# A convolution of two layers computed as three short filters over even and odd blocks, in place of one filter of five slots

## The chip, the cores and the metric

The kernel runs on one core of one Trainium2 chip. The metric is the device time of one execution in microseconds; of three runs of the kernel before the median is 1592.81 us (1592.79 to 1595.31).

## The reference

```
for two layers (conditioned convolution, then a product over the feature dimension):
    out = x                                   # 64 batch entries, 64 channels, 1024 positions
    for typ in ('same', 'upsample', 'same', 'downsample'):
        s = style @ mw.T + mb                 # each batch entry has its own weights
        weight = SCALE * w * s ; weight = weight * rsqrt(sum(weight^2) + EPS)
        out = conv(out, weight) + b           # 3 taps; up by 2 then blur, blur then down by 2
    x = x + FFN(out)
layer 0: FFN(y) = y @ identity.T              # 1024 x 1024
layer 1: FFN(y) = y @ W_base.T + b_base + sum_e alpha_e * (y @ A_e.T @ B_e.T) * 2   # 4 experts, softmax gate
```

All is float32. Away from the ends of the 1024 positions, the four convolutions of one batch entry are together one linear filter, so they can be composed into one.

## The kernel before

The batch is worked in 32 pairs of entries (`j`), the two entries of a pair being halves `h` = 0 and 1. Two input rows, even and odd positions, lie over the 128 partitions (64 channels each): `xraw` holds x in partitions 0 to 63 and x moved by one position in 64 to 127, so every second column gives a pair of neighbouring positions. The output is laid out alike: a product of 128x128 with 512 columns gives all 1024 positions of a half.

Every float32 factor is split in a high part of the type float32r and the rest (`_h`, `_l`), and `three` (lines 1099 to 1101) issues three products: high by high, high by rest, rest by high.

For each pair TensorE composes the filter in stages, with ScalarE making the high parts and VectorE the low ones between them: `stage_v`, `stage_u`, `stage_t`. `stage_t` leaves five slots of 64 columns in PSUM for each half (`comp_ps[h]`). `t_high` (ScalarE, L509) and `t_low` (VectorE, L803, L976, L977) scale them by the style and place them in `tw[h]`: slot `u` is a matrix of 128x128 for shift `u`, whose second 64 columns are copies of the first, moved across the partitions. Then `stage_conv(j, h)` runs five slots, each `three` with 512 columns, over `x_h[h]`, `x_l[h]`. `x_h` is written by ScalarE (L488, `x_high`), `x_l` by GpSimd (L348, `split_low`). `conv_scaled` (ScalarE, L523) takes the result out of PSUM with scale and bias into `conv[h]`, GpSimd's `put_edge` (L355) writes the two positions at each end, which are computed apart in the prologue (`ends_0` to `ends_4`), and `stage_turn` (L1364) transposes it on TensorE for the FFN product.

What follows for each half:

```
for u in range(NSH):                                   # NSH = 5
    last = three(conv_ps[h][:, :], flat(tw[h][:, 0, u, :, :]), flat(tw[h][:, 1, u, :, :]),
                 x_h[h][:, u:u + HL], x_l[h][:, u:u + HL], u == 0, u == NSH - 1)
```

Each engine has its program written out by hand, and an engine works strictly in its own order, held by semaphores. TensorE's body for pair `j` puts the FFN products of pair `j-1` (`ffn_chunk`, 8 chunks x 2 column blocks in layer 0; `ffn_row`, 3 blocks in layer 1) between the composing stages of pair `j`, to give the other engines time: in layer 0 four times three products of 512 columns lie between `stage_t` and `stage_conv`, in layer 1 five times three of 354 or 352, and `stage_turn` is two times three (layer 0) behind the second half's convolution. VectorE's body is `compose_low` (`v_low`, `z_low`, `t_low`, `w2_low` for the next pair; in layer 1 also `gates`), then `turned_low`, `ffn_result` for pair `j-1`, `turned_low`.

In layer 0 the pairs 2 to 8 and the last carry one step each of layer 1's preparation: `prep(step)` on VectorE and ScalarE, `prep_between` and `prep_after` on TensorE. Before the loop of each layer stands a prologue, in which pair 0, the composing of pair 1, the ends and the transposed FFN weights (`turn_weights`, `fw_high`, `fw_low`) are interleaved.

SP issues all loads and stores of x: `load_x(j)` when `x_ready` says that pair `j-1` is split (xraw is a single buffer), then it waits for the FFN result of pair `j-2`, stores it and loads `xres` for `j-1`.

## Time and profile before

| | |
|---|---|
| profiled execution | 1594.2 us, its span 1592.3 us |
| median of the runs | 1592.81 us |
| TensorE busy | 1559.0 us, 98% |
| VectorE busy | 798.6 us, 50% |
| ScalarE busy | 577.3 us, 36% |
| GpSimd busy | 206.4 us, 13% |
| body of one pair | 22.47 us in layer 0, 23.50 us in layer 1 |

Busy time is time in which an engine has an instruction under way. Matmuls overlap in the records (a product starts before the one ahead of it has drained), so what a product costs in a run of them is the distance of their starts, not its length. A row of a timeline that stands for several instructions says xN; an idle time ahead of it is in brackets, with what ended it.

### The profile page before, as it was taken

How to read it: one execution, taken by the hardware profiler on the slowest of the kernel's cores; microseconds unless marked ns; L12 is line 12 of the kernel's file. 1: busy time of each engine (PE TensorE's matmuls, PEld its weight loads, DVE VectorE, ACT ScalarE, POOL GpSimd, SP SyncE). 2: the span in 40 equal slices, each digit the busy share in tenths (PEclk: the TensorE clock that was granted, in tenths of full speed). 3: DMA queues.
4: the chain of work that ended last, by engine and by line, in shares of the span. 5: the costliest groups of instructions: out<-in, count | busy, mean ns of one | idle time of the engine just before them, and what ended most of it. 6: DMA issues, size and time to landing. Idle time of an engine off the chain costs nothing.

```text
span 1592.3 us, 25445 instructions
## 1 busy us (share of the span) xinstructions
PE 1559.0 (98%) x8503; PEld 1376.3 (86%) x8503; DVE 798.6 (50%) x2061; ACT 577.3 (36%) x1291; POOL 206.4 (13%) x280
## 2 busy tenths in 40 slices
PE   5999999999999999999999999999999999999998
PEld 4688888888888888888868999999999999999998
DVE  7645655454444444454555554454555455445443
ACT  3323442334333333333333333333334333333332
POOL 1101010111011101111100110111111011011010
PEclk9999998999999999999999999999999999999999
DMA  4352332332333233333262333332332333333331
GB/s 103 99 117 82 106 80 64 95 101 83 102 83 105 81 104 79 105 92 92 66 185 67 79 96 88 79 105 79 83 101 79 99 85 89 96 79 99 86 79 66
DMA packets 54331, 145.66 MB, mean 91 GB/s; under 512 B 17233, under 2 KB 19345, under 8 KB 54306
## 3 DMA queue, kind: packets, MB, share of 16 engines
q1 hardware_dynamic: 53616, 144.96, 33.4%
q10 hardware_dynamic: 690, 0.37, 0.1%
q8 instruction: 15, 0.25, 0.1%
q14 instruction: 10, 0.08, 0.0%
HBM read 111.75 MB, written 33.55 MB: 91 GB/s over the span
## 4 chain that ended last, share of the span: by engine, by line
PE 93%; DVE 3%; issue 2%; DMA 1%; ACT 1%; POOL 0%; SPq 0%; DVEq 0%; POOLq 0%
PE bank L1099 29%; PE bank L1101 29%; PE bank L1100 28%; PE bank L1364 4%; PE bank L1246 1%; DMA xraw<-x_dram 1%; PE bank L1310 0%; PE bank L1281 0%; DVE fw_l L884 0%; DMA win<-in_L_cond_weights_dram 0%; PE bank L1176 0%; PE bank L1178 0%; PE bank L1300 0%; PE bank L1370 0%; DVE win L907 0%
## 5 line engine op out<-in xcount | busy, mean ns | idle before, releaser
L1099 PE MATMUL bank<-fw_h,ct_h 128*128 128x512 f32 (+2 forms) x1280 | 458.9, 358 | 0.6 <-DVE xout L856 0.5
L1100 PE MATMUL bank<-fw_l,ct_h 128*128 128x512 f32 (+2 forms) x1280 | 450.3, 352 | 0.0
L1101 PE MATMUL bank<-fw_h,ct_l 128*128 128x512 f32 (+2 forms) x1280 | 449.3, 351 | 0.0
L348 POOL TENSOR_TENSOR x_l<-xraw,x_h 128x512 fp32r<-128x512 f32 x128 | 165.8, 1317 | 1258.1 <-ACT x_h L488 1258.1
L992 DVE TENSOR_TENSOR ct_l<-bank,ct_h 128x384 fp32r<-128x384 f32 (+1 forms) x256 | 96.2, 417 | 390.3 <-ACT ct_h L536 389.8
L1101 PEld LDWEIGHTS bank<-fw_h,ct_l 128*128 128x128 f32 x1280 | 241.0, 188 | 22.7
L1099 PEld LDWEIGHTS bank<-fw_h,ct_h 128*128 128x128 f32 x1280 | 241.2, 188 | 20.8 <-issue 1.0
L1100 PEld LDWEIGHTS bank<-fw_l,ct_h 128*128 128x128 f32 x1280 | 241.6, 189 | 16.4
L1099 PE MATMUL bank<-x_h,tw 128*128 128x512 f32 x640 | 253.1, 395 | 0.5 <-DVE tw L977 0.5
L1101 PE MATMUL bank<-x_h,tw 128*128 128x512 f32 x640 | 252.8, 395 | 0.0
L1100 PE MATMUL bank<-x_l,tw 128*128 128x512 f32 x640 | 251.8, 394 | 0.0
L523 ACT ACTIVATE conv_buf<-bank,beta,lam 128x508 f32<-128x508 f32 x128 | 99.6, 778 | 400.1 <-PE bank L1101 400.1
L503 ACT ACTIVATE z_h<-bank,lam_pairs 64x256 fp32r<-64x256 f32 (+1 forms) x256 | 113.6, 444 | 214.1 <-PE bank L1101 194.9
L961 DVE TENSOR_SCALAR z_f<-bank,lam_pairs 64x256 f32<-64x256 f32 (+1 forms) x256 | 115.2, 450 | 146.4 <-PE bank L1101 138.7
L536 ACT CAST ct_h<-bank 128x384 fp32r<-128x384 f32 (+1 forms) x256 | 86.7, 375 | 174.4 <-PE bank L1246 61.6
L1101 PEld LDWEIGHTS bank<-x_h,tw 128*128 128x128 f32 x640 | 120.4, 188 | 27.9
L1099 PEld LDWEIGHTS bank<-x_h,tw 128*128 128x128 f32 x640 | 120.4, 188 | 27.9 <-DVE tw L977 0.9
L1100 PEld LDWEIGHTS bank<-x_l,tw 128*128 128x128 f32 x640 | 120.5, 188 | 27.4 <-issue 0.2
L803 DVE SCALAR_TENSOR_TENSOR tw<-bank,s_all,tw 128x320 fp32r<-128x320 f32 x128 | 70.5, 551 | 95.3 <-ACT tw L509 93.0
L856 DVE TENSOR_TENSOR xout<-bank,xres 128x352 f32<-128x352 f32 (+1 forms) x160 | 86.8, 576 | 40.9 <-PE bank L1246 40.9
L976 DVE CAST tw<-tw 64x640 fp32r<-64x640 f32 x128 | 88.8, 694 | 4.4
L488 ACT CAST x_h<-xraw 128x512 fp32r<-128x512 f32 x128 | 78.3, 660 | 4.8 <-DMA xraw<-x_dram 3.4
(203 smaller groups left out, 1783.1 us busy)
## 6 DMA issues: line engine op xcount, KB each, us to landing
xraw<-in_x_dram SPq DMA_DIRECT2D x32, 512.0 KB, 5.0
xres<-in_x_dram SPq DMA_DIRECT2D x32, 512.0 KB, 3.9
x_dram<-xout SPq DMA_DIRECT2D x32, 512.0 KB, 2.9
xraw<-x_dram SPq DMA_DIRECT2D x32, 512.0 KB, 5.0
xres<-x_dram SPq DMA_DIRECT2D x32, 512.0 KB, 3.9
out_dram<-xout SPq DMA_DIRECT2D x32, 512.0 KB, 2.9
xraw<-in_x_dram SPq DMA_DIRECT2D x32, 511.5 KB, 6.5
xraw<-x_dram SPq DMA_DIRECT2D x32, 511.5 KB, 6.5
```

The source lines that it names most:

```text
L348: nc.gpsimd.tensor_tensor(x_l[h][:, PAD:PAD + HL], src, x_h[h][:, PAD:PAD + HL].bitcast(F32), ALU.subtract).then_inc(s["x_ready"], 1)
L488: nc.scalar.copy(x_h[h][:, PAD:PAD + HL], xraw[:, h, :].rearrange("p (m q) -> p m q", q=2)[:, :, 0]).then_inc(s["x_hi"], 1)
L503: nc.scalar.activation(z_h[half(i), h, 0:4 - i, :], u_ps[half(h), i::2, :], ACT.Copy, scale=lam1_pairs[half(h), bass.ds(j, 1)]).then_inc(s ...
L523: nc.scalar.activation(conv[h][:, 2:HL - 2], conv_ps[h][:, 2:HL - 2], ACT.Identity, scale=lam4[:, bass.ds(2 * j + h, 1)], bias=beta[:, bas ...
L536: nc.scalar.copy(ct_h[:, ks, h, :], conv_ps[h][:, :].rearrange("p (k o) -> p k o", o=C)[:, ks, :]).then_inc(s["ct_hi"], 1)
L856: v.tensor_tensor(xout[:, lo:hi], ffn_ps[e][:, skip:skip + hi - lo], xres[:, lo:hi], ALU.add).then_inc(s["ffn_out"], 1)
L961: v.tensor_scalar(z_f[half(i), h, 0:4 - i, :], u_ps[half(h), i::2, :], lam1_pairs[half(h), bass.ds(j, 1)], None, ALU.mult).then_inc(s["z_o ...
L976: v.tensor_copy(tw[h][half(1), :, :, 1, :], tw[h][half(0), :, :, 0, :].bitcast(F32))
L992: v.tensor_tensor(ct_l[:, ks, h, :], conv_ps[h][:, :].rearrange("p (k o) -> p k o", o=C)[:, ks, :], ct_h[:, ks, h, :].bitcast(F32), ALU.su ...
L1099: mm(out, wh, xh, start=start, stop=False, skip_group_check=True)
L1100: mm(out, wh, xl, start=False, stop=False, skip_group_check=True)
L1101: return mm(out, wl, xh, start=False, stop=stop, skip_group_check=True)
```

## The change

The filter of five slots on 512 columns is computed in the way of a fast two-part filter. The 512 columns are taken as even and odd ones (256 each). Three short filters are run, each over 256 columns:

- P: the sum filter, slots `G0`, `G1` (sums of neighbouring slots) and 4, over the odd columns `o` (nine products into `comp_ps[h]`, the bank which held the composed slots).
- over the difference `d[:, 0]` of neighbouring columns, slots 0, 2, 4 (nine products into the first half of `conv_ps[h]`).
- over `d[:, 1]`, slots 1 and 3 (six products into the second half).

The even output columns are P plus the second result, the odd ones P minus the third. So:

- `tw` has 8 slots for 5; three of them are sums of neighbouring slots. VectorE now makes the scaled slots in float32 (`t_f`, which lies in the buffer `conv[h]`), adds, subtracts ScalarE's high part, and makes all copies between the partition halves. It does the first two steps for both halves before the others.
- GpSimd makes the differences (`neighbours`) ahead of ScalarE's high part, and the low parts of both `d` and `o`. It does this for pair `j+1` once the filters of pair `j` are ready; the edges of pair `j` go first.
- ScalarE makes the high parts of `x` for pair `j+1` in two pieces, around `sum_scaled`, which takes P out of PSUM with scale and bias into every second column of `conv[h]`. VectorE's new `conv_out` adds the other two results.
- In VectorE's body `conv_out(j, 0)` stands ahead of `w2_low` and `prep(step)`, `conv_out(j, 1)` behind them; in layer 1 `gates` stands ahead of both.
- TensorE waits for P scaled ahead of `stage_v(1)` and `stage_u(1)` in the prologue. Semaphores of the ends are merged.

```diff
 # VectorE
                 def t_low(j):
                     for h in range(2):
+                        full = t_f[h]
+                        dve.wait_ge(s["t_acc"], 2 * j + h + 1)
+                        v.tensor_scalar(full[:, 0:NSH, :], comp_ps[h][:, 0:NSH * C].rearrange("p (u c) -> p u c", c=C),
+                                        s_all[:, 0, bass.ds(2 * j + h, 1)], None, ALU.mult).then_inc(s["g_made"], 1)
+                        dve.wait_ge(s["g_made"], 4 * j + 2 * h + 1)
+                        v.tensor_tensor(full[:, G0:SLOTS, :], full[:, 0:3, :], full[:, 1:4, :], ALU.add).then_inc(s["g_made"], 1)
+                    for h in range(2):
                         dve.wait_ge(s["t_hi"], 2 * j + h + 1)
-                        low(tw[h][:, 1, :, 0, :], comp_ps[h][:, 0:NSH * C].rearrange("p (u c) -> p u c", c=C),
-                            s_all[:, 0, bass.ds(2 * j + h, 1)], tw[h][:, 0, :, 0, :]).then_inc(s["t_lo"], 1)
+                        v.tensor_tensor(tw[h][:, 1, :, 0, :], t_f[h][:, :, :], tw[h][:, 0, :, 0, :].bitcast(F32),
+                                        ALU.subtract).then_inc(s["t_lo"], 1)
                         dve.wait_ge(s["t_lo"], 2 * j + h + 1)
                         v.tensor_copy(tw[h][half(1), :, :, 1, :], tw[h][half(0), :, :, 0, :].bitcast(F32))
-                        v.tensor_copy(tw[h][half(0), :, 1:NSH, 1, :], tw[h][half(1), :, 0:NSH - 1, 0, :].bitcast(F32)
-                                      ).then_inc(s["t_ready"], 1)
+                        v.tensor_copy(tw[h][half(0), :, 1:NSH, 1, :], tw[h][half(1), :, 0:NSH - 1, 0, :].bitcast(F32))
+                        v.tensor_copy(tw[h][half(0), :, G0:SLOTS:G1 - G0, 1, :],
+                                      tw[h][half(1), :, 0:GM + 1:GM, 0, :].bitcast(F32)).then_inc(s["t_ready"], 1)
+                def conv_out(j, h):
+                    dve.wait_ge(s["p_scaled"], 2 * j + h + 1)
+                    dve.wait_ge(s["conv_acc"], 2 * j + h + 1)
+                    even = conv[h][:, 2:HL - 2:2]
+                    stt(out=conv[h][:, 3:HL - 1:2], in0=conv_ps[h][:, QL + 1:2 * QL - 1], scalar=neg4[...],
+                        in1=even, op0=ALU.mult, op1=ALU.add)
+                    stt(out=even, in0=conv_ps[h][:, 1:QL - 1], scalar=lam4[...],
+                        in1=even, op0=ALU.mult, op1=ALU.add).then_inc(s["c_mid"], 1)
...
                 def body(j, step=None, composed=False):
                     if not composed:
-                        compose_low(j, ly["lora"])
-                    elif ly["lora"]:
+                        compose_low(j)
+                    if ly["lora"]:
                         gates(j - 1)
+                    conv_out(j, 0)
+                    if not composed:
+                        w2_low(ly, j + 1)
                     if step is not None:
                         prep(step)
+                    conv_out(j, 1)
                     turned_low(j, 0)
 # GpSimd
+                def neighbours(j):
+                    pool.wait_ge(s["x_load"], 32 * j + 32)
+                    for h in range(2):
+                        m0, m1 = (xraw[:, h, at:at + L].rearrange("p (n e q) -> p e n q", e=2, q=2)[:, :, :, 0] for at in (0, 2))
+                        nc.gpsimd.tensor_tensor(d_f[h][:, :, :], m0, m1, ALU.subtract).then_inc(s["d_made"], 1)
+                def split_low(j):
+                    for h in range(2):
+                        pool.wait_ge(s["x_hi"], 2 * j + h + 1)
+                        nc.gpsimd.tensor_tensor(d_l[h][:, :, 1:QL + 1], d_f[h][:, :, :], d_h[h][:, :, 1:QL + 1].bitcast(F32),
+                                                ALU.subtract)
+                        nc.gpsimd.tensor_tensor(o_l[h][:, 1:QL + 1], xraw[:, h, 2:L:4], o_h[h][:, 1:QL + 1].bitcast(F32),
+                                                ALU.subtract).then_inc(s["x_ready"], 1)
+                def body(j, last=False):
+                    pool.wait_ge(s["t_ready"], 2 * j + 2)
+                    edges(j)
+                    if not last:
+                        x_next(j)          # waits t_ready again, then neighbours(j + 1), split_low(j + 1)
 # ScalarE
+                def x_high(j, h, first=False):
+                    if not first:
+                        act.wait_ge(s["conv_acc"], 2 * j + h - 1)
+                    act.wait_ge(s["d_made"], 2 * j + h + 1)
+                    nc.scalar.copy(o_h[h][:, 1:QL + 1], xraw[:, h, 2:L:4])
+                    nc.scalar.copy(d_h[h][:, :, 1:QL + 1], d_f[h][:, :, :]).then_inc(s["x_hi"], 1)
+                def sum_scaled(j, h):
+                    act.wait_ge(s["p_acc"], 2 * j + h + 1)
+                    nc.scalar.activation(conv[h][:, 2:HL - 2:2], comp_ps[h][:, 1:QL - 1], ACT.Identity, ...
 # body of ScalarE: v_high, z_high, t_high, (gate_exp), sum_scaled(j,0), w2_high, x_high(j+1,0), prep, sum_scaled(j,1), x_high(j+1,1), ...
 # TensorE
+                    for i, slot in enumerate((G0, G1, 4)):
+                        last = conv_tap(h, comp_ps[h][:, 0:QL], slot, o_h[h][:, i:i + QL], o_l[h][:, i:i + QL], i == 0, i == 2)
+                    last.then_inc(s["p_acc"], 1)
                     if not first:
                         pe.wait_ge(s["ct_ready"], 4 * j)
-                    for u in range(NSH):
-                        last = three(conv_ps[h][:, :], flat(tw[h][:, 0, u, :, :]), flat(tw[h][:, 1, u, :, :]),
-                                     x_h[h][:, u:u + HL], x_l[h][:, u:u + HL], u == 0, u == NSH - 1)
+                    for i, slot in enumerate((0, 2, 4)):
+                        conv_tap(h, conv_ps[h][:, 0:QL], slot, d_h[h][:, 0, i:i + QL], d_l[h][:, 0, i:i + QL], i == 0, i == 2)
+                    for i, slot in enumerate((1, 3)):
+                        last = conv_tap(h, conv_ps[h][:, QL:2 * QL], slot, d_h[h][:, 1, i:i + QL], d_l[h][:, 1, i:i + QL], False, i == 1)
```

## Rows read from the trace of the kernel before

**Rows 1.** The page: busy time and share by engine; the chain that ended last.
```profile
PE 1559.0 (98%) x8503; PEld 1376.3 (86%) x8503; DVE 798.6 (50%) x2061; ACT 577.3 (36%) x1291; POOL 206.4 (13%) x280
...
PE bank L1099 29%; PE bank L1101 29%; PE bank L1100 28%; PE bank L1364 4%; PE bank L1246 1%; DMA xraw<-x_dram 1%; PE bank L1310 0%; PE bank L1281 0%; DVE fw_l L884 0%; DMA win<-in_L_cond_weights_dram 0%; PE bank L1176 0%; PE bank L1178 0%; PE bank L1300 0%; PE bank L1370 0%; DVE win L907 0%
```

**Rows 2.** View by stretches: length, busy us (instructions) per engine, clock, DMA share, GB/s.
```profile
500.86:523.33 22.47, 22.47 (x116) 18.79 (x115) 10.14 (x24) 8.28 (x18) 3.12 (x4) 1.00 0.34 93
1196.49:1219.99 23.50, 23.50 (x143) 22.11 (x142) 11.78 (x33) 8.64 (x21) 3.11 (x4) 1.00 0.33 89
```

**Rows 3.** Timeline of TensorE, both layers: start, length, engine, line, tile.
```profile
507.70 0.28 PE L1100 MATMUL bank<-z_l,w_h 128*128 128x256 f32 x1
...
508.88 0.28 PE L1101 MATMUL bank<-z_h,w_l 128*128 128x256 f32 x1
...
511.55 0.19 PEld L1099 LDWEIGHTS bank<-x_h,tw 128*128 128x128 f32 x1
...
511.78 0.39 PE L1099 MATMUL bank<-x_h,tw 128*128 128x512 f32 x1
...
518.49 0.39 PE L1101 MATMUL bank<-x_h,tw 128*128 128x512 f32 x1
...
520.11 1.04 PE L1364 MATMUL bank<-ident,conv_buf 128*128 128x128 f32 x8
...
1210.32 0.39 PE L1099 MATMUL bank<-x_h,tw 128*128 128x512 f32 x1
```

**Rows 4.** Timeline of VectorE, then ScalarE, in the same bodies.
```profile
509.81 0.92 DVE L976 CAST tw<-tw 64x640 fp32r<-64x640 f32 x1
510.74 0.44 DVE L977 CAST tw<-tw 64x512 fp32r<-64x512 f32 x1
...
511.79 0.49 DVE L976 CAST tw<-tw 64x640 fp32r<-64x640 f32 x1
512.29 0.42 DVE L977 CAST tw<-tw 64x512 fp32r<-64x512 f32 x1
...
521.26 1.02 DVE L992 TENSOR_TENSOR ct_l<-bank,ct_h 128x384 fp32r<-128x384 f32 x2 [7.90 <-ACT ct_h L536]
...
507.04 1.22 ACT L488 CAST x_h<-xraw 128x512 fp32r<-128x512 f32 x2
508.57 0.53 ACT L509 ACTIVATE tw<-bank,s_all 128x320 fp32r<-128x320 f32 x1 [0.30 <-PE bank L1101]
...
1207.47 0.53 ACT L509 ACTIVATE tw<-bank,s_all 128x320 fp32r<-128x320 f32 x1 [0.33 <-PE bank L1101]
```

**Rows 5.** Groups by line and shape: count | busy, mean ns | idle before, releaser.
```profile
L348 POOL TENSOR_TENSOR x_l<-xraw,x_h 128x512 fp32r<-128x512 f32 x128 | 165.8, 1317 | 1258.1 <-ACT x_h L488 1258.1
...
L803 DVE SCALAR_TENSOR_TENSOR tw<-bank,s_all,tw 128x320 fp32r<-128x320 f32 x128 | 70.5, 551 | 95.3 <-ACT tw L509 93.0
...
L961 DVE TENSOR_SCALAR z_f<-bank,lam_pairs 64x256 f32<-64x256 f32 x128 | 61.8, 483 | 142.3 <-PE bank L1101 138.7
...
L966 DVE TENSOR_TENSOR z_l<-z_f,z_h 128x256 fp32r<-128x256 f32 x128 | 48.7, 422 | 2.2
```

**Rows 6.** Stretches of VectorE's `prep` steps 0, 2, 3, 6; last, one at start.
```profile
111.69:115.49 3.80, 3.77 (x11) 1.00 0.96 194
161.27:170.22 8.95, 5.37 (x17) 1.00 0.37 76
183.93:190.17 6.24, 5.82 (x18) 1.00 0.57 115
263.96:274.18 10.22, 7.37 (x14) 1.00 0.37 75
76.00:80.00 4.00, 2.90 (x6) 0.57 0.70 202
```

**Rows 7.** Timelines in the two prologues: VectorE, ScalarE.
```profile
48.69 0.22 DVE L746 TENSOR_TENSOR beta<-blur_n,bias 128x64 f32<-128x64 f32 x1
...
803.81 1.21 ACT L488 CAST x_h<-xraw 128x512 fp32r<-128x512 f32 x2 [3.39 <-DMA xraw<-x_dram]
```

More of the change, by code:

```diff
@@ L215, in build @@
         names = ("w_load mw_load params f_load0 f_load1 f_load2 f_load3 modt_acc modt s_acc s_ready w2_acc w2_ready d_acc dvar_ready dsqrt "
[L216 to L219 removed]
+                 "wt_acc wt_ready ends_in ends_acc "
+                 "edge_ready bias_acc bias_ready fw_acc fw_hi fw_ready chain "
+                 "x_load res_load d_made x_hi x_ready w2_hi w2_low v_acc v_hi v_ready u_acc z_hi z_own z_ready t_acc g_made t_hi "
+                 "t_ready blur_ready base_ready w1_placed mst_ready split_hi split_ready t_lo p_acc p_scaled conv_acc c_mid c_edge ct_acc ct_hi ct_ready ffn_acc ffn_out stored").split()
         for n, ly in enumerate(layers):
@@ L374, in _ @@
                                             ALU.subtract).then_inc(s["split_ready"], 1)
-                body(0, True)
-                with pool.Fori(1, NPAIR) as j:
+                neighbours(0)
+                split_low(0)
+                x_next(0)
+                pool.wait_ge(s["edge_ready"], 1)
+                if ly is not layers[0]:
+                    pool.wait_ge(layers[0]["s"]["ct_acc"], 2 * NPAIR)
+                edges(0)
+                with pool.Fori(1, NPAIR - 1) as j:
                     body(j)
+                body(NPAIR - 1, True)
         @block.scalar
@@ L480, in fw_high @@
                         nc.scalar.copy(dst, bank[6 + g % 2][:, :].rearrange("p (k e) -> p k e", k=4)).then_inc(s["fw_hi"], 1)
-                def x_high(j, first=False):
-                    act.wait_ge(s["x_load"], 32 * j + 32)
+                def x_high(j, h, first=False):
                     if not first:
-                        act.wait_ge(s["conv_acc"], 2 * j)
-                    for h in range(2):
-                        nc.scalar.copy(x_h[h][:, PAD:PAD + HL],
-                                       xraw[:, h, :].rearrange("p (m q) -> p m q", q=2)[:, :, 0]).then_inc(s["x_hi"], 1)
+                        act.wait_ge(s["conv_acc"], 2 * j + h - 1)
+                    act.wait_ge(s["d_made"], 2 * j + h + 1)
+                    nc.scalar.copy(o_h[h][:, 1:QL + 1], xraw[:, h, 2:L:4])
+                    nc.scalar.copy(d_h[h][:, :, 1:QL + 1], d_f[h][:, :, :]).then_inc(s["x_hi"], 1)
                 def v_high(j):
@@ L580, in _, with body @@
                 t_high(1)
-                def body(j, step=None, composed=False):
+                def body(j, step=None, composed=False, last=False):
                     if not composed:
-                        compose_high(j, ly["lora"])
-                    elif ly["lora"]:
+                        compose_high(j)
+                    if ly["lora"]:
                         gate_exp(j - 1)
-                    conv_scaled(j, 0)
+                    sum_scaled(j, 0)
+                    if not composed:
+                        w2_high(ly, j + 1)
+                    if not last:
+                        x_high(j + 1, 0)
                     if step is not None:
                         prep(step)
-                    conv_scaled(j, 1)
+                    sum_scaled(j, 1)
+                    if not last:
+                        x_high(j + 1, 1)
                     if ly["lora"]:
@@ L1035, in _ @@
                     prep_bias(ly, link, 2)
+                    conv_out(0, 0)
                     g = 6
@@ L1044, in _ @@
                     ends_0()
+                    conv_out(0, 0)
                     fw_low(0, 2)
@@ L1051, in _ @@
                 fw_low(g, g + 2 + 2 * n)
+                conv_out(0, 1)
                 g += 2 + 2 * n
@@ L1347, in stage_t, with conv_tap @@
                         last.then_inc(s["t_acc"], 1)
+                def conv_tap(h, out, slot, xh, xl, start, stop):
+                    return three(out, flat(tw[h][:, 0, slot, :, :]), flat(tw[h][:, 1, slot, :, :]), xh, xl, start, stop)
                 def stage_conv(j, h, first=False):
```

140 lines of the change are left out of this document (67 added, 73 removed).

## The prediction

> **What bounds the kernel now.** I read four views. The page's first part has TensorE busy 98% of the span, VectorE 50%; its chain of waits runs 93% through TensorE, 86% on the lines of `three` [rows 1]. The view by stretches says the same of one pair of batch entries: TensorE is busy for all of a 22.47 us body of layer 0 and a 23.50 us body of layer 1, VectorE for 10.14 and 11.78 us [rows 2]. So TensorE work taken out is time won, unless something late leaves a gap. The timelines show how late things are. In layer 0 ScalarE takes up the first composed filter (`t_high`) at 508.57; call that T. TensorE loads the first filter slot for the convolution at 511.55 (T+2.98) and multiplies at 511.78 (T+3.21), without a gap [rows 3]. VectorE finished this filter's last copy, `tw` L977, at 510.74+0.44 = 511.18, T+2.6 [rows 4]. The filter chain is thus early by under 0.4 us. In layer 1 T is 1207.47 and the first multiply is at 1210.32, T+2.85 [rows 3, 4].
>
> **TensorE: what goes.** The thirty 512-column products of a pair start from 511.78 to 518.49, 29 steps: 0.2313 us each. In a run of 256-column products, 507.70 to 508.88, ten steps take 1.18 us: 0.118 each [rows 3]. Before, a half costs 15 x 0.2313 = 3.47 us; after, eight slots of three products, 24 x 0.118 = 2.83. Saved: 0.638 x 128 halves = **-81.6 us**. Weight loads (0.19 us in the records) start every 0.118 us in that same stage and hold nothing up, so their number, 24 for 15, is free here; if forty-eight in a row did not keep that pace, at 3.47/24 = 0.145 us each the whole gain would be gone. I take 0.118: it is the same shape. The low end of the saving is therefore zero, the high end this.
>
> **VectorE: the filter chain (`t_low`).** It now does, in this order: scale slots of half 0 out of PSUM (128x320), add three slots (128x192), the same for half 1, and only then for half 0 subtract (128x512), copy 64x1024, 64x512, 64x256. Prices [rows 5]: ops with a pointer scalar out of PSUM are 0.483 at 256 columns and 0.551 at 320, so 0.55, and the slope is 1.06 ns a column; the two-tensor op is 0.422 at 256 columns, with that slope 0.35 for 192 and 0.69 for 512. Casts undisturbed are 0.42 for 512 and 0.49 for 640 [rows 4], slope 0.55 ns, so 0.70 for 1024 and 0.28 for 256. The Trainium skill (VectorE: DVE Perf Modes, the TRN2 errata) gives (N+151)/0.96 ns for the two-tensor op, 0.691 us at 512; a 128x512 one between SBUF tiles is in no row, and the sum would not move.
>
> Laid out: start T+0.03; scale 0.58; add 0.97; second scale overlaps 0.04 and ends 1.48; add 1.87; ScalarE's `t_high` copy (128x512, as `x_h`, two in 1.22 us [rows 4]) begins near 1.1 and is seen at 1.89; subtract 2.59; casts 3.3, 3.75, 4.05; TensorE sees it at 4.15 and multiplies at 4.27. The stall is 4.27-3.21 = 1.06 us in layer 0 and 4.27-2.85 = 1.42 in layer 1. Thirty pairs of each layer meet it (pairs 0 and 1 are composed ahead): 31.8+42.6 = **+74.4 us**. Bounds: all prices by the closest overlap, 3.85 at TensorE (0.65, 1.0: +50 us); the 1024 copy at the disturbed speed of the 640 one, 0.92 beside GpSimd [rows 4], about 0.6 more per half, a chain of 4.9 (+110 us). GpSimd is however moved away: it starts pair j+1 only when both filters of pair j are ready, so the chain runs undisturbed, and I take the middle. Half 1 is ready at T+6.3 and needed at 7.1: covered.
>
> **What follows the convolution.** The convolution of half 0 is T+4.27 to 7.1, half 1 to 9.9. FFN products from 518.72 to 520.11, 1.39 us, stand ahead of the eight transposes (1.04 us) [rows 3], half 1's four come 0.4 later, so `c_mid` of half 1 is due at 11.7. It is now two VectorE ops (128x254 scalar ops, 0.48 each) after `conv_acc` at 10.2: done 11.2 (in their place ScalarE took 0.78 before). ScalarE must have scaled P before: it waits in `x_high(j+1,0)` for GpSimd's difference (edges 0.6, then 1.32 for 128x512 [rows 5]: T+8.4), copies 1.0, scales P by 9.9. Hidden, by 0.5 us; a GpSimd difference of over 2.1 us would break it. The six GpSimd ops take some 6.6+0.6 us, done near T+13.6, far before the next T. SP's `load_x` waits on the same `x_ready` half a period earlier: free. ScalarE's second `x_high` ends at 11.3, before the transposes that `turned_high` waits for. In layer 1 the `gates` (2.3 us) stand ahead of `conv_out`, T+6.3 to 8.6: also hidden. Priced at **0**, bounds -0 and +0.5 x 60.
>
> **The preparation of layer 1.** In pairs 2 to 8 and 31 of layer 0, `prep(step)` stood in 7.9 us of VectorE idle time ahead of `ct_l` [rows 4]. Now it stands between `conv_out(j,0)` with `w2_low` (done T+8.9) and `conv_out(j,1)`, which must begin by 10.7. Only 1.8 us are covered; TensorE's transposes wait for the rest. Each stretch from first to last op (four of the eight are in [rows 6]), and the stall: step 0, 3.8 us, 2.0; step 2, where 5.15 us follow ScalarE's root (T+10.4), 4.9; step 3, 6.2 us, 4.4; step 4, 3.4 us, 1.6; pair 31, 0.6. In steps 1, 5 and 6 TensorE itself waits at `prep_between` (T+7.1) for the first VectorE results (T+9.65, 9.4, 10.35): 2.5, 2.3 and 3.3, and step 6 has 6.2 us more behind it, 2.8. Sum 24.4. Bounds: 12 (half of it beside waits that exist anyway) and 40. Beside GpSimd a cast took 0.92 instead of 0.49 [rows 4], and GpSimd now works from T+6.4 to 13.6, over the prep ops; I add 3: **+27 us**. The Trainium skill (GPSIMD Engine Reference, Specifications) names ops with two SBUF inputs as disturbed too; no row of before shows it. By it the squares and blur steps would stretch as well, some 5 us more.
>
> **The two prologues.** Layer 0: `stage_v(1)` now waits for P scaled, P needs `bias_ready` 3. VectorE made the bias at 48.9 [rows 7]; it comes 3.1 us later, as `t_low(0)` is longer (two adds, two small copies, wider ops). ScalarE scales at 52.1 to 52.7, `stage_v(1)` starts at 52.9 where it was at 49.6, +3.3, and +0.2 more at `conv_out` before `ends_3`. GpSimd writes edges only after pair 1's split, which takes four ops behind ScalarE's four copies: +1.3. Layer 1: x lands at 803.8 [rows 7] and GpSimd's difference now stands ahead of ScalarE's copy; chain to the first filter +3.3, +1.5 after. With the four convolutions' saving, counted above, put back (2 x 1.28): 4.8+4.8+2.6 = **+12 us**, bounds 4 and 20.
>
> **Sum.** -81.6+74.4+27+12 = **+32 us**. The profiled execution took 1594.2 us, span 1592.3 and 1.9 around it: 1626. The median of the runs, 1592.81, is 1.4 below it: **1625 us**.
>
> **The rivals.**
> A. The chain fits better than laid out: GpSimd's disturbance gone, VectorE's ops overlap, and the stall falls under 0.4 us. For it: baseline's first cast lost 0.43 us to GpSimd. Against: the reorder puts half 1's two ops (0.9 us) ahead of half 0's, and the slots are 8 for 5. Stalls then cost under 20 us: 1592.8-81.6+20+35 = 1566. Chance 0.13; it is the faster side.
> B. P's detour: GpSimd's difference reads xraw with a stride of four and comes after 2.1 us, or ScalarE is late. The end is then `c_mid`. At 2.6 us each +0.6 x 60 = +36: 1661. Against: the split at stride two costs 1.317 [rows 5]. Chance 0.1.
> C. TensorE's clock. In 76 to 80 it was granted at 0.57 of full, behind gaps of over 1 us in the prologue [rows 6], so partly its lower level of 1.2 GHz. Stalls of 3 to 6 us in the prep steps might do that seven times; at some 2 us each 1625+14 = 1639. Against: bodies before and after are full. Chance 0.07.
> D. The saving and the new stall balance and prep's cost is half hidden: 1592.8-81.6+60+12+9 = 1592, no change. Chance 0.06.
>
> The likeliest, 0.64, is 1625. Range **1590 to 1652**: it takes the chain at 50 to 95 us and the prep at its bounds; A and most of B lie outside. A measurement of this kernel tells apart about 0.2%, 3.2 us. Of D's 0.06, 0.02 is faster and 0.04 the same; of the likeliest's own lower tail 0.01 and 0.02. Faster 0.13+0.03 = 0.16, same 0.06, slower 0.78.
>
> **What would show it.** Right: the convolution's products 0.118 us apart; a TensorE gap of about 1 us each pair ahead of its first product, put down to VectorE's last copy of `tw`; gaps before the transposes in pairs 2 to 8 put down to `conv_out`; VectorE's share near 67% (2.3 us more a half: 798.6+292 of 1623), GpSimd's near 28%. Wrong: no gap at the convolution (A), a gap at the transposes in every pair (B), a clock under 0.98 over layer 0 (C), or products further apart than 0.12 us.

## The result, and the profile after

The changed kernel takes 1698.75 us in the median of four runs (1697.24 to 1700.48), beside 1592.81 of the kernel before: a ratio of 1.066, 95% interval 1.064 to 1.068. It is slower, as forecast, but by 106 us instead of 32; the range ended at 1652.

The page first (busy time; the chain of waits; two groups, with count | busy us, mean ns | idle before, releaser):

```profile
PE 1527.6 (90%) x9655; PEld 1394.5 (82%) x9655; DVE 1199.4 (71%) x2703; ACT 624.5 (37%) x1419; POOL 459.2 (27%) x537
...
PE 58%; DVE 31%; issue 7%; ACT 1%; DMA 1%; POOL 1%; DVEq 1%; SPq 0%; POOLq 0%; ACTq 0%
PE bank L1160 18%; PE bank L1162 17%; PE bank L1161 17%; DVE conv_buf L1012 4%; DVE tw L1018 4%; DVE w_l L841 3%; PE bank L1433 3%; DVE tw L1022 3%; DVE gate L1059 2%; DVE tw L1023 2%; DVE conv_buf L1015 2%; DVE conv_buf L1039 1%; DVE conv_buf L1037 1%; DVE tw L1024 1%; DVE gate L1063 1%
...
L1433 PE MATMUL bank<-ident,conv_buf 128*128 128x128 f32 x512 | 77.7, 285 | 69.0 <-DVE conv_buf L1039 68.3
L841 DVE SCALAR_TENSOR_TENSOR w_l<-w_st,lam,w_h 128x128 fp32r<-128x128 f32 x132 | 132.9, 1046 | 0.0
```

TensorE's share has fallen from 98% to 90%, and VectorE holds 31% of the chain of waits where TensorE's lines held nearly all [rows 1]. VectorE and GpSimd have the shares that were forecast, within five points (71% and 27%; 67% and 28% forecast). What was not: `w_l`, an operation that the change does not touch, has a mean of 1046 ns, and the transposes of all pairs together (L1433) waited 68.3 us for `conv_out` (L1039).

One body of each layer, by stretches, and then the pairs 1 to 9 (from transposes to transposes) of the kernel before and the changed one, in which layer 1 is prepared. Columns as in [rows 2]; the last two rows of each kernel read: length, busy us of TensorE (its instructions), clock:

```profile
594.00:615.98 21.98, 21.49 (x133) 18.76 (x132) 15.79 (x35) 9.07 (x21) 7.02 (x9) 1.00 0.35 95
1200.97:1226.02 25.05, 22.91 (x159) 22.22 (x159) 18.54 (x44) 9.24 (x22) 6.97 (x9) 1.00 0.31 84
```
```profile
96.26:295.23 198.97, 198.93 (x1009) 0.97 0.31 86
```
```profile
100.79:354.49 253.70, 207.38 (x1154) 0.90 0.25 67
```

Layer 0's steady body is 21.98 us, 0.49 less than before; layer 1's is 25.05, 1.55 more [rows 2]. The eight bodies of the preparation grew by 54.7 us. Three stages are thus to be explained. From here on a body is the distance between the first transposes of neighbouring pairs.

**Layer 0, the filter.** VectorE's and TensorE's timeline, T being 607.17 (the forecast laid VectorE's first row at T+0.03):

```profile
607.20 0.55 DVE L1012 TENSOR_SCALAR conv_buf<-bank,s_all 128x320 f32<-128x320 f32 x1 [0.82 <-PE bank L1162]
607.78 0.36 DVE L1015 TENSOR_TENSOR conv_buf<-conv_buf 128x192 f32<-128x192 f32 x1
608.06 0.55 DVE L1012 TENSOR_SCALAR conv_buf<-bank,s_all 128x320 f32<-128x320 f32 x1
608.64 0.36 DVE L1015 TENSOR_TENSOR conv_buf<-conv_buf 128x192 f32<-128x192 f32 x1
608.91 0.69 DVE L1018 TENSOR_TENSOR tw<-conv_buf,tw 128x512 fp32r<-128x512 f32 x1
609.64 0.69 DVE L1022 CAST tw<-tw 64x1024 fp32r<-64x1024 f32 x1
610.34 0.42 DVE L1023 CAST tw<-tw 64x512 fp32r<-64x512 f32 x1
610.68 0.28 DVE L1024 CAST tw<-tw 64x256 fp32r<-64x256 f32 x1
```
```profile
611.02 0.38 PE L1160 MATMUL bank<-o_h,tw 128*128 128x256 f32 x1 [0.49 <-DVE tw L1024]
611.24 0.28 PE L1161 MATMUL bank<-o_l,tw 128*128 128x256 f32 x1
611.36 0.28 PE L1162 MATMUL bank<-o_h,tw 128*128 128x256 f32 x1
...
616.86 0.39 PE L1160 MATMUL bank<-fw_h,ct_h 128*128 128x512 f32 x1
```

The order is the one laid out. The first product holds the second off for 0.22 us; the other 47 follow at 0.12 each (611.24 to 616.86, where the next work starts). The gap ahead of the first is 0.49 us and put down to the last copy.

**Layer 1, behind the filter.** VectorE, then GpSimd, then TensorE:

```profile
1219.02 1.39 DVE L1059 TENSOR_SCALAR gate<-gate 128x4 f32<-128x4 f32 x1
...
1221.07 0.63 DVE L1063 TENSOR_SCALAR gate<-gate 128x4 f32<-128x4 f32 x1
...
1223.22 1.97 DVE L841 SCALAR_TENSOR_TENSOR w_l<-w_st,lam,w_h 128x128 fp32r<-128x128 f32 x2
...
1225.50 0.47 DVE L1039 SCALAR_TENSOR_TENSOR conv_buf<-bank,lam,conv_buf 128x254 f32<-128x254 f32 x1
```
```profile
1219.05 2.63 POOL L362 TENSOR_TENSOR d_f<-xraw 128x512 f32<-128x512 f32 x2
1222.97 1.20 POOL L367 TENSOR_TENSOR d_l<-d_f,d_h 128x512 fp32r<-128x512 f32 x1 [1.29 <-ACT d_h L521]
1224.12 0.91 POOL L369 TENSOR_TENSOR o_l<-xraw,o_h 128x256 fp32r<-128x256 f32 x1
```
```profile
1226.02 0.66 PE L1433 MATMUL bank<-ident,conv_buf 128*128 128x128 f32 x4 [1.30 <-DVE conv_buf L1039]
```

L1059 is a VectorE operation on 128x4 numbers. It takes 1.39 us and ends at 1220.41; the first of GpSimd's two differences, half of 2.63 us, ends near 1220.37. The next such one, L1063, ends at 1221.70, GpSimd's second difference at 1221.68. The two `w_l`, 0.36 us each in the kernel before, take 1.97 together and end at 1225.19, GpSimd's L369 at 1225.03. Behind all this stands the last `conv_out`, and TensorE's transposes wait 1.30 us for it. From this a hypothesis: an operation of some kinds on VectorE, once issued, stands until the GpSimd instruction under way ends.

### The profile page after: what moved, and what is told of

Read it like the earlier page. It is cut to its first block, busy times and chain, and to the rows that moved or that the text cites. A ratio compares the mean times of both kernels' runs of the same rounds, so it can differ in the third digit from the quotient of the medians.

```text
span 1695.4 us, 29216 instructions
## 1 busy us (share of the span) xinstructions
PE 1527.6 (90%) x9655; PEld 1394.5 (82%) x9655; DVE 1199.4 (71%) x2703; ACT 624.5 (37%) x1419; POOL 459.2 (27%) x537
## 4 chain that ended last, share of the span: by engine, by line
PE 58%; DVE 31%; issue 7%; ACT 1%; DMA 1%; POOL 1%; DVEq 1%; SPq 0%; POOLq 0%; ACTq 0%
PE bank L1160 18%; PE bank L1162 17%; PE bank L1161 17%; DVE conv_buf L1012 4%; DVE tw L1018 4%; DVE w_l L841 3%; PE bank L1433 3%; DVE tw L1022 3%; DVE gate L1059 2%; DVE tw L1023 2%; DVE conv_buf L1015 2%; DVE conv_buf L1039 1%; DVE conv_buf L1037 1%; DVE tw L1024 1%; DVE gate L1063 1%
## 5 line engine op out<-in xcount | busy, mean ns | idle before, releaser
L367 POOL TENSOR_TENSOR d_l<-d_f,d_h 128x512 fp32r<-128x512 f32 x128 | 155.5, 1215 | 129.2 <-ACT d_h L521 125.3
L1160 PE MATMUL bank<-d_h,tw 128*128 128x256 f32 x640 | 182.8, 286 | 0.0
L1161 PE MATMUL bank<-d_l,tw 128*128 128x256 f32 x640 | 181.8, 284 | 0.0
L1162 PE MATMUL bank<-d_h,tw 128*128 128x256 f32 x640 | 181.7, 284 | 0.0
L362 POOL TENSOR_TENSOR d_f<-xraw 128x512 f32<-128x512 f32 x128 | 168.5, 1337 | 48.6 <-DMA xraw<-x_dram 32.4
L1160 PE MATMUL bank<-o_h,tw 128*128 128x256 f32 x384 | 118.2, 308 | 45.2 <-DVE tw L1024 45.2
L1046 DVE TENSOR_TENSOR ct_l<-bank,ct_h 128x384 fp32r<-128x384 f32 (+1 forms) x256 | 99.2, 417 | 62.1 <-ACT ct_h L564 61.7
L541 ACT CAST tw<-conv_buf 128x512 fp32r<-128x512 f32 x128 | 79.4, 621 | 171.4 <-DVE conv_buf L1015 171.4
L1433 PE MATMUL bank<-ident,conv_buf 128*128 128x128 f32 x512 | 77.7, 285 | 69.0 <-DVE conv_buf L1039 68.3
L841 DVE SCALAR_TENSOR_TENSOR w_l<-w_st,lam,w_h 128x128 fp32r<-128x128 f32 x132 | 132.9, 1046 | 0.0
L1160 PEld LDWEIGHTS bank<-o_h,tw 128*128 128x128 f32 x384 | 74.2, 193 | 68.0 <-DVE tw L1024 67.3
L1433 PEld LDWEIGHTS bank<-ident,conv_buf 128*128 128x128 f32 x512 | 61.6, 145 | 82.9 <-DVE conv_buf L1039 76.8
```

Of the source, the lines that this page charges most:

```text
L362: nc.gpsimd.tensor_tensor(d_f[h][:, :, :], m0, m1, ALU.subtract).then_inc(s["d_made"], 1)
L367: nc.gpsimd.tensor_tensor(d_l[h][:, :, 1:QL + 1], d_f[h][:, :, :], d_h[h][:, :, 1:QL + 1].bitcast(F32), ALU.subtract)
L541: nc.scalar.copy(tw[h][:, 0, :, 0, :], t_f[h][:, :, :]).then_inc(s["t_hi"], 1)
L841: return stt(out=dst, in0=ps, scalar=lam, in1=high.bitcast(F32), op0=ALU.mult, op1=ALU.subtract)
L1046: v.tensor_tensor(ct_l[:, ks, h, :], conv_ps[h][:, :].rearrange("p (k o) -> p k o", o=C)[:, ks, :], ct_h[:, ks, h, :].bitcast(F32), ALU.su ...
L1160: mm(out, wh, xh, start=start, stop=False, skip_group_check=True)
```

## The experiments

Three theories. H (hold): the above, and it makes most of the 74 us that were missed. V (volume): VectorE has simply too much to do behind the convolution, GpSimd or not. P (place): the preparation steps stand in the wrong place. Bodies of all kernels, in us, from the timelines; "start" is from the span's begin to the first transposes, "between" from layer 0's last to layer 1's first. Times and ratios are from medians, the stages from the one profiled execution of each kernel:

| kernel | time | ratio (95%) | start | pairs 1 to 9 | body, layer 0 | between | body, layer 1 |
|---|---|---|---|---|---|---|---|
| before | 1592.8 | 1 | 76.3 | 199.0 | 22.47 | 56.5 | 23.50 |
| changed | 1698.8 | 1.066 | 82.4 | 253.7 | 21.98 | 68.4 | 25.05 |
| 1 GpSimd small | 1610.7 | 1.010 (1.007-1.013) | 79.5 | 225.4 | 21.98 | 60.2 | 23.40 |
| 2 prep ahead | 1680.6 | 1.054 (1.051-1.057) | 83.5 | 237.5 | 21.98 | 68.0 | 25.04 |
| 3 GpSimd in quarters | 1638.5 | 1.028 (1.025-1.031) | 85.3 | 239.7 | 21.98 | 68.0 | 23.40 |
| 4 `w2_low` behind | 1653.5 | 1.037 (1.034-1.040) | 82.2 | 253.7 | 21.98 | 66.0 | 23.54 |
| 5 GpSimd later | 1620.8 | 1.017 (1.015-1.019) | 83.7 | 223.6 | 21.98 | 66.7 | 23.39 |
| 6 = 5 + 2 | 1604.5 | 1.007 (1.005-1.009) | 82.2 | 208.6 | 21.98 | 67.2 | 23.40 |
| 7 = 6 + third copy on ScalarE | 1586.7 | 0.995 (0.993-0.997) | 81.6 | 205.5 | 21.78 | 67.3 | 23.19 |
| 8 third copy alone | 1680.7 | 1.055 (1.053-1.057) | 81.6 | 256.0 | 21.78 | 66.1 | 24.64 |
| 9 = 7, all copies shared | 1563.1 | 0.981 (0.980-0.983) | 80.8 | 201.5 | 21.38 | 62.1 | 22.80 |

### 1. GpSimd's large operations on one column

```diff
-                        nc.gpsimd.tensor_tensor(d_f[h][:, :, :], m0, m1, ALU.subtract)
+                        nc.gpsimd.tensor_tensor(d_f[h][:, :, 0:1], m0[:, :, 0:1], m1[:, :, 0:1], ALU.subtract)
```

and the same for `d_l` and `o_l`.

> GpSimd's six large operations of a pair work on one column each and the rest of d and of the low parts stays zero (the computation of d, d_l and o_l is left out). Theory H: a VectorE instruction that needs a second SBUF input, or runs at two elements a cycle, stands until the GpSimd instruction under way ends. Then w_l (1.05 us mean in the changed kernel) falls to its 0.36 of before, the two gate operations of 1.39 and 0.63 us to 0.23, TensorE's wait of 1.3 us ahead of the transposes in layer 1 goes, the body of layer 1 falls from 25.05 to about 23.1 us and that of layer 0 from 21.98 to about 21.7; with a third off the preparation, 1610 us in all. Rival V: VectorE simply has too much work in the right order (71% busy); then w_l falls but the body of layer 1 stays above 24.5 us and the time above 1675.

Measured: 1610.66 us. `w_l` and the gates in the kernel with small GpSimd operations (timeline; then the group):

```profile
1207.98 0.25 DVE L1060 TENSOR_SCALAR gate<-gate 128x4 f32<-128x4 f32 x1
...
1208.90 0.23 DVE L1064 TENSOR_SCALAR gate<-gate 128x4 f32<-128x4 f32 x1
```
```profile
L842 DVE SCALAR_TENSOR_TENSOR w_l<-w_st,lam,w_h 128x128 fp32r<-128x128 f32 x132 | 41.5, 356 | 0.0
```

H holds: 88 us of the 106 go with GpSimd's length. By stage: layer 1's body loses 1.65 us (47.7 in the thirty; the first of them took 23.54 in the changed kernel), pairs 1 to 9 28.3, "between" 8.2, the start 2.9. V is out: VectorE issues the same. The time was met, the stages less well: both bodies are 0.3 us longer than expected (21.98 and 23.40 for 21.7 and 23.1), so the rest won more than was thought. And GpSimd's work, not only its hold on VectorE, is gone here; 3 and 5 separate the two.

### 2. The preparation steps ahead of `conv_out(j, 0)`

```diff
                     if ly["lora"]:
                         gates(j - 1)
+                    if step is not None and step < PREPS:
+                        prep(step)
                     conv_out(j, 0)
```

> VectorE's preparation steps 0 to 6 stand ahead of conv_out(j,0) instead of between the two conv_out. If the place of the preparation is what costs (theory P), TensorE's waits at prep_between (4.0, 4.2 and 5.1 us) nearly go and those ahead of the transposes shrink by the 2.6 us or more that w_l and conv_out stood ahead: pairs 1 to 9 of layer 0 take 230 us for 253.7, 1675 us in all. If only the amount of VectorE work counts, the same 1698.

Measured: 1680.64 us; pairs 1 to 9 lose 16.2 us where some 24 were expected, no other stage over half a microsecond but the start (+1.1). TensorE's three waits at `prep_between` are gone, as expected, but six of 3.9 to 6.0 us are left ahead of the transposes. P is true for 16 us, and no more.

### 3. GpSimd's operations in pieces of 128 columns

```diff
-                        nc.gpsimd.tensor_tensor(d_f[h][:, :, :], m0, m1, ALU.subtract)
+                        for c in range(0, QL, P):
+                            nc.gpsimd.tensor_tensor(d_f[h][:, :, c:c + P], ...)     # and d_l, o_l
```

(The pieces have 128 elements a partition each.) All is computed, and GpSimd has more to do, not less. Two ways of being disturbed differ here: held until the instruction ends (H), or sharing a port for as long as both are busy (S).

> The same GpSimd work in instructions of 128 columns instead of 512 and 256. Theory H (held until the end of the instruction under way): an instruction of VectorE is held for one short instruction at most, so the gate operation of 1.39 us falls under 0.7 and the pair of w_l from 2.4 and 2.0 us under 1.5; body of layer 1 about 24.2, 1665 us in all. Rival S (the two engines share a port's bandwidth, column by column): w_l and the gate operations keep their length within 10%, and the time stays 1690 to 1710, GpSimd being busy longer.

Measured: 1638.47 us, beyond what H said. VectorE, then GpSimd, in the kernel with pieces:

```profile
1237.44 0.48 DVE L1066 TENSOR_SCALAR gate<-gate 128x4 f32<-128x4 f32 x1
...
1238.59 0.23 DVE L1070 TENSOR_SCALAR gate<-gate 128x4 f32<-128x4 f32 x1
...
1239.20 0.57 DVE L1075 CAST zcat<-za 128x32 fp32r<-128x32 f32 x1
...
1240.98 0.95 DVE L848 SCALAR_TENSOR_TENSOR w_l<-w_st,lam,w_h 128x128 fp32r<-128x128 f32 x2
```
```profile
1237.47 3.51 POOL L364 TENSOR_TENSOR d_f<-xraw 128x128 f32<-128x128 f32 x8
1240.94 1.72 POOL L372 TENSOR_TENSOR d_l<-d_f,d_h 128x128 fp32r<-128x128 f32 x4
```

The gate that took 1.39 us beside an instruction of 1.3 takes 0.48 beside instructions of 0.44 (3.51/8), and a pair of `w_l` 0.95 where it took 1.97. The delay follows the length of the single GpSimd instruction, not GpSimd's busy time: it is a hold, and S is out. Not every meeting costs: the second gate operation kept its 0.23 us amid the pieces, in all pairs (mean 230 ns), while the cast on 128x32 behind it took 0.57, and 0.18 in the changed kernel, where it met no GpSimd instruction. What decides between the two stays open. The body of layer 1 is 23.40, as without GpSimd's work at all. Pairs 1 to 9 keep 14 of their 28 us, and where GpSimd's work itself is waited for, its greater length costs (start +2.9).

### 4. `w2_low` behind `conv_out(j, 1)`

```diff
-                    if not composed:
+                    if not composed and step is not None:
                         w2_low(ly, j + 1)
...
                     conv_out(j, 1)
+                    if not composed and step is None:
+                        w2_low(ly, j + 1)
```

Here the held operation stays held, but nobody waits for it.

> w2_low stands behind conv_out(j,1) where there is no preparation step. It took 2.0 us of the time between the two conv_out in layer 1 and 2.4 in layer 0. If it is what makes the last conv_out late, TensorE's 1.3 us wait ahead of the second half's transposes goes: layer 1 about 23.9 us a body, layer 0 about 21.7, 1658 us in all. If the gates alone make it late, the body of layer 1 stays above 24.7 and the time above 1688.

Measured: 1653.46 us. The first gate operation is held as before (1276 ns in the mean, 1309 in the changed kernel), `w_l` less (772 for 1046), and the body of layer 1 is 23.54: of its 1.65 us, 1.51 were `w_l` in the way of `conv_out(j, 1)`. Layer 0, expected at 21.7, stays at 21.98: there `w_l` was in nobody's way. The gates lose 1.16 and 0.40 us by the hold (1.39 and 0.63 for 0.23) and cost 0.14. In pairs 1 to 9, where nothing was edited, nothing changed.

### 5. GpSimd starts behind `conv_out(j, 1)`

```diff
 # GpSimd, body
                     if not last:
+                        pool.wait_ge(s["c_mid"], 2 * j + 2)
                         x_next(j)
 # ScalarE: x_high(j + 1, 0) between the parts of turned_high(j), x_high(j, 1) behind v_high(j)
```

> All of GpSimd's work is done, but for pair j+1 it starts only when both conv_out of pair j are ready; ScalarE's high parts move with it, half 0 between the two parts of turned_high, half 1 behind the next v_high. Theory H (VectorE held by GpSimd): the gates, w_l and the preparation run at their undisturbed lengths as with GpSimd's work taken out, bodies 23.4 us in layer 1 and 21.98 in layer 0, pairs 1 to 9 near 227 us, the transition unchanged: 1698.75 - 30 x 1.65 - 27 = 1622 us. Rival V (the amount of work, with the new order no better): bodies of layer 1 above 24 us, because the late split then meets v_low, z_low or ScalarE's v_high.

Measured: 1620.81 us.

```profile
L841 DVE SCALAR_TENSOR_TENSOR w_l<-w_st,lam,w_h 128x128 fp32r<-128x128 f32 x132 | 41.6, 357 | 0.0
...
L1059 DVE TENSOR_SCALAR gate<-gate 128x4 f32<-128x4 f32 x32 | 7.4, 230 | 1.1
```

`w_l` and the gates have the lengths they have alone, the body of layer 1 is 23.39 and pairs 1 to 9 lose 30.1 us, with the whole of GpSimd's work kept at full length. The prologues keep their times within 2 us. Keeping the two engines apart costs nothing in the bodies.

### 6. Both: later, and the preparation ahead

> As the kernel before it, and the preparation steps 0 to 6 ahead of conv_out(j,0). The place of the preparation costs beside the hold: the earlier place alone gained 18 us. If the two are separate, another 10 to 18 us: 1606. If that gain was only the hold avoided, 1620.

Measured: 1604.52 us, 1.5 below what was expected: the two causes add up (15.0 us less in pairs 1 to 9 than in 5, 16.2 in 2 against the changed kernel).

### 7. The third copy on ScalarE

To 6 is added:

```diff
-                        v.tensor_copy(tw[h][half(0), :, G0:SLOTS:G1 - G0, 1, :],
-                                      tw[h][half(1), :, 0:GM + 1:GM, 0, :].bitcast(F32)).then_inc(s["t_ready"], 1)
 # ScalarE, behind both t_high copies
+                    for h in range(2):
+                        act.wait_ge(s["t_lo"], 2 * j + h + 1)
+                        nc.scalar.copy(tw[h][half(0), :, G0:SLOTS:G1 - G0, 1, :],
+                                       tw[h][half(1), :, 0:GM + 1:GM, 0, :].bitcast(F32)).then_inc(s["t_third"], 1)
```

> As the kernel before it, and the third copy (the sum slots 5 and 7) on ScalarE, beside VectorE's other two. Theory C: in every body what is left of the stall is the length of VectorE's filter chain, so 0.28 us less in it is 0.28 us less a body: 21.70 and 23.12 us, 60 bodies x 0.28 = 17 us, 1590 us in all. Rival: ScalarE's copy is later than VectorE's two (0.47 us for 64x256 behind its two high parts), the bodies gain under 0.1 us and the time stays at 1605.

Measured: 1586.67 us, 0.5% below the kernel before (ratio 0.993 to 0.997). Both bodies lose 0.20 us where 0.28 was expected: in the changed kernel the third copy started before the second had ended (610.68, 610.34+0.42) and ended 0.20 behind it. That is its net price.

### 8. The third copy alone, on the changed kernel

> The changed kernel with nothing but the third copy on ScalarE. Under theory C layer 0 gains 0.28 us a body (21.70). In layer 1 the stall is ahead of the transposes, at the end of a VectorE sequence that is itself 0.57 us shorter, so about as much there as well, 24.5 a body: 1698.75 - 22 x 0.28 - 30 x 0.5 - some 4 = 1674. Should layer 1 not move at all, its bound is GpSimd's or ScalarE's timetable and not VectorE's: 1690.

Measured: 1680.74 us, 18.0 less than the changed kernel, where 25 were expected. Layer 0 gains the same 0.20; layer 1 gains 0.41, twice 0.20, since the copies of both halves leave VectorE's queue ahead of the gates and `conv_out`, and there VectorE is late. Pairs 1 to 9 did not gain (+2.3). The third copy on VectorE is thus a cost, the smaller one: 18 of 106.

### 9. All copies shared out

In 7, VectorE still copies 64x1024 and 64x512. Here it copies the low parts alone, ScalarE the high ones, which it can do while VectorE subtracts:

```diff
 # ScalarE, t_high, for each half
                         nc.scalar.copy(tw[h][:, 0, :, 0, :], t_f[h][:, :, :]).then_inc(s["t_hi"], 1)
+                        act.wait_ge(s["t_hi"], 2 * j + h + 1)
+                        nc.scalar.copy(tw[h][half(1), 0, :, 1, :], tw[h][half(0), 0, :, 0, :].bitcast(F32))
+                        nc.scalar.copy(tw[h][half(0), 0, 1:NSH, 1, :], tw[h][half(1), 0, 0:NSH - 1, 0, :].bitcast(F32))
                         act.wait_ge(s["t_lo"], 2 * j + h + 1)     # then the third copy, as in 7
 # VectorE
-                        v.tensor_copy(tw[h][half(1), :, :, 1, :], tw[h][half(0), :, :, 0, :].bitcast(F32))
+                        v.tensor_copy(tw[h][half(1), 1, :, 1, :], tw[h][half(0), 1, :, 0, :].bitcast(F32))
 # and likewise the second
```

> This is the kernel of the third-copy-and-later-GpSimd experiment (1586.7 us) with the copies of the filter between the partition halves shared out: VectorE copies only the low parts (64x512 and 64x256), ScalarE the high parts (64x512, 64x256) and the third copy of both parts. Theory 1, the filter chain is still what TensorE waits for: the third copy has left a wait of 0.28 us in every body of layer 0 and 0.6 us in every body of layer 1 (18.8 us over 30 bodies), and VectorE's two copies after its subtraction now take some 0.7 us instead of 1.1, ScalarE's three, which start while VectorE subtracts, end at about the same time. The chain shortens by 0.4 to 0.5 us: bodies of 21.5 and 22.8 us instead of 21.78 and 23.19, a time near 1567 us. Rival: something else is as late as the filter (ScalarE's own queue, in which the copy of the second half's filter, P's scaling and the high part of x now stand 0.6 us later, and with it GpSimd's low parts), and the bodies stay within 0.1 us: 1583 to 1590 us, or above 1590 if ScalarE becomes the bound.

Measured: 1563.05 us (1559.01 to 1567.11, five runs), ratio 0.981 (0.980 to 0.983). VectorE, ScalarE and TensorE in layer 0:

```profile
590.13 0.55 DVE L1018 TENSOR_SCALAR conv_buf<-bank,s_all 128x320 f32<-128x320 f32 x1 [0.82 <-PE bank L1169]
...
591.85 0.69 DVE L1024 TENSOR_TENSOR tw<-conv_buf,tw 128x512 fp32r<-128x512 f32 x1
592.57 0.42 DVE L1028 CAST tw<-tw 64x512 fp32r<-64x512 f32 x1
593.00 0.29 DVE L1029 CAST tw<-tw 64x256 fp32r<-64x256 f32 x1
```
```profile
591.76 0.62 ACT L544 CAST tw<-tw 64x512 fp32r<-64x512 f32 x1
592.39 0.41 ACT L545 CAST tw<-tw 64x256 fp32r<-64x256 f32 x1
592.70 0.40 ACT L547 CAST tw<-tw 64x256 fp32r<-64x256 f32 x1
```
```profile
593.35 0.39 PE L1167 MATMUL bank<-o_h,tw 128*128 128x256 f32 x1
```

From VectorE's first operation to the first product there are now 3.22 us, against 3.82 in the changed kernel, and the product has no gap ahead of it. Bodies of 21.38 and 22.80 us are 1.09 and 0.70 below those of before; of the 1.28 us of TensorE work all but 0.19 are won in layer 0 and all but 0.58 in layer 1, where a gap of 0.23 us for the filter is left. (The profiled executions of 7 and 9 lie 30 us apart, the medians 24; the stages of the table are from the profiled ones.)

## Why the prediction failed

**Term by term.** With the body table, the forecast's terms can be read off (measured = what a stage grew by, with the forecast's 1.28 us of saved products a pair put back):

| term | forecast | changed kernel | GpSimd small (1) |
|---|---|---|---|
| products | -81.6 | -81.6 | -81.6 |
| chain to the filter, 30 + 30 pairs | +74.4 | 0.79 x 30 + 1.18 x 30 = +59 | +59 |
| behind the convolution, layer 1 | 0 | 749.7 - 702.0, thirty bodies = +47.7 | 0 |
| preparation | +27 | 54.7 + 10.2 - 6.3 = +58.6 | +30.3 |
| two prologues | +12 | 6.1 + 12.0 + 2.6 = +20.7 | +9.5 |
| sum | +32 | +104 | +17 |

(In the preparation 10.2 is eight bodies' saved products and 6.3 their chain, 8 x 0.79. The chain in layer 1 is 23.40 - 23.50 + 1.28, from the kernels whose transposes don't wait. The products' term is taken over from the forecast; what their distance missed (0.12 for 0.118 us) is in the chain's 59. The spans of the profiled executions differ by 103.1 and 15.7 us, the medians by 106 and 18; the sums meet them within 2 us.) One step failed: **the price of VectorE's operations beside GpSimd's**. It was set to nothing behind the convolution ("hidden, by 0.5 us") and to 3 us in the preparation. It was 47.7, and 28 with the lower clock that came along. The prologues lose 11 us as well when GpSimd's work is taken out, but that is not shown to be the hold: VectorE's operations are longer there by some 3 and 4 us in all, experiment 5 wins next to nothing there, and the rest may be GpSimd's own length on the path, or the clock (TensorE was granted 0.89 in "between", 0.99 in experiment 1). Beside the kernel with GpSimd's work taken out the forecast was 14 us too high, not 74 too low: the chain's 15.

**What the row had said.** A cast of `tw` took 0.92 us in place of 0.49 [rows 4], and the prediction read this as a "disturbed speed". GpSimd's row of that moment stood beside it:

```profile
507.78 2.59 POOL L348 TENSOR_TENSOR x_l<-xraw,x_h 128x512 fp32r<-128x512 f32 x2 [19.34 <-ACT x_h L488]
```

GpSimd's instruction ended at 510.37, the cast at 510.73, which is 0.36 later, less than the 0.49 of the next such cast, which met nothing. With the experiments behind it, this reads as a hold and no speed: its price is not a share of the operation, it is what is left of the other engine's instruction, up to 1.3 us, for an operation on four columns as for one of 640. The forecast also had the two collide by design: "GpSimd now works from T+6.4 to 13.6", over the whole of `gates`, `conv_out`, `w2_low` and `prep`.

The forecast named one page of the Trainium skill (GPSIMD Engine Reference, Specifications), which says which operations contend and not for how long, and put it at "some 5 us more". Another page, not drawn on, has the price: the Trainium skill (SBUF — State Buffer, Who interferes with whom) says that the pair of ports which the two engines share goes to whoever issues first "for the whole instruction" and the other blocks, where VectorE's instruction has two SBUF inputs or runs in a two-port mode. The runs here agree on which operations are held and that they are held to the end of the other's instruction; in which mode the casts ran, and whether GpSimd is held in its turn, no run here shows. Held were `w_l` (two inputs in SBUF, 1046 ns instead of 356), and casts and scalar operations from SBUF to SBUF, down to 128x4; `conv_out`, one of whose inputs lies in PSUM, was not (0.47 us at 617.45 and 617.84, beside GpSimd's instruction from 617.34 to 618.29).

**Behind the convolution, layer 0.** That bound held, but by luck of place: `w_l` took 2.40 us there too,

```profile
615.13 2.40 DVE L841 SCALAR_TENSOR_TENSOR w_l<-w_st,lam,w_h 128x128 fp32r<-128x128 f32 x2
```
```profile
613.51 2.65 POOL L362 TENSOR_TENSOR d_f<-xraw 128x512 f32<-128x512 f32 x2
616.19 1.19 POOL L367 TENSOR_TENSOR d_l<-d_f,d_h 128x512 fp32r<-128x512 f32 x1
```

and `conv_out(j, 1)`, done at 618.31, was just in time for the transposes of its half (the eight start at 618.25, the first four need the other half), since in layer 0 no gates stand ahead. In layer 1 2.3 us of gates, 1.5 more by the hold, use up what cover there was. Rival B (0.1) named the place, `c_mid` late in every pair, at +36 us where +47.7 came, and its sign, a gap at the transposes; but in the steady bodies the gap came in layer 1 alone, and by another cause: B's own, P scaled late by GpSimd's difference, doesn't show (experiment 4 leaves that difference where it is, and the body is 23.54).

**The filter's chain.** Its mechanism was right and its size off: the sign "about 1 us each pair" was 0.49 in layer 0 by the records and 0.84 in layer 1, while the bodies lost 0.79 and 1.18, against 1.06 and 1.42. It was laid out as ending at T+4.05 on VectorE and multiplied at T+4.27; the trace has T+3.79 (610.68+0.28) and T+3.85, the lower bound "by the closest overlap". Three of VectorE's eight operations start 0.08 to 0.09 before the one ahead has ended, where one overlap was laid out, and TensorE followed the last copy after 0.06, where 0.22 was laid out. The rest of a body's loss, 0.79 less 0.64, is the first product after a gap, which holds the next off for 0.22 us instead of 0.118 (0.10), and the distance of the other 47, 0.1196 instead of 0.118 (0.08).

**The preparation and the clock.** Rival C (clock) was given 0.07, as a case by itself. It came as a part. In the eight bodies TensorE was busy 207.4 us, where 198.9 - 10.2 = 188.7 would have been at the old clock; idle it was 46.3. The granted clock fell from 0.97 to 0.90. A gap ahead of the transposes and FFN products behind it:

```profile
197.27 1.12 PE L1433 MATMUL bank<-ident,conv_buf 128*128 128x128 f32 x4 [7.00 <-DVE conv_buf L1039]
...
199.46 0.63 PE L1160 MATMUL bank<-fw_h,ct_h 128*128 128x512 f32 x1
199.89 0.63 PE L1161 MATMUL bank<-fw_l,ct_h 128*128 128x512 f32 x1
```
```profile
194.40:201.20 6.80, 3.93 (x12) 3.26 (x13) 4.50 (x18) 0.48 (x1) 0.00 (x0) 0.50 0.00 0
```

They are 0.43 apart where 0.23 is usual, at the granted clock of 0.50, the lower of the two levels (1.2 GHz). In this stage the clock was at that level in nine stretches of the changed kernel, 51 us in all. Eight of them begin in a gap of 3.8 to 7.9 us or within 1.0 us behind it. The ninth, 296.8 to 303.6, begins in a row of products on 4 and 32 columns without a gap, and it is no cost of the change: the kernel before has it at the same place, TensorE being busy throughout:

```profile
243.60:253.80 10.20, 10.20 (x35) 9.11 (x36) 0.74 (x2) 0.73 (x2) 0.00 (x0) 0.50 0.19 61
```

Half of TensorE's busy time in such stretches is what the lower level cost: an estimate of 20.3 us in the changed kernel (half of 40.5) and of 5.1 in the one before. So of the 207.4 - 188.7 = 18.7 us of longer busy time some 15 are the clock, and the rest, about 3, belongs to the 17 gaps themselves (each ends with a product drained and begins with one that holds the next off). Of the 65 us that the preparation lost (46.3 + 18.7), some 15 were thus paid at the lower clock, most of them behind the gaps. In 6, then in 1, the same 1154 products:

```profile
101.05:309.66 208.61, 196.01 (x1154) 0.96 0.30 82
```
```profile
97.26:322.63 225.37, 199.34 (x1154) 0.95 0.28 76
```

The forecast's 24.4 us for the steps' place has the size of what is left without the hold, 30.3 in experiment 1, of which 10.6 are longer busy time (199.3 - 188.7). It isn't borne out as the price of the place: moving the steps ahead won 16 us in 2 and 15 in 6. What set the clock was not tried by itself. Over all kernels more idle time goes with a lower clock (idle 0.0, 12.6, 26.0 and 46.3 us; clock 0.97, 0.96, 0.95, 0.90 in the kernel before, 6, 1 and the changed one), but not strictly: 5 was idle for 21.8 us at 0.93.

**Saving and weight loads.** Forty-eight loads in a row kept 0.12 us a product (5.62 us for 47); the low end "no saving" is out.

**Open.** "Between" is still 67 us in 7 and 62 in 9 where 56.5 was; the waits there (3.9 us for the filter in 7) were read, but no kernel took them away. Of the 5 us that 9 took off it as well, 2.1 are idle time of TensorE (13.1 to 11.0) and 3.1 busy time (54.2 to 51.1), at a granted clock of 0.96 where it was 0.91.
